# Cross-attention and quantised feed-forward: probabilities turned through device memory, attention one step later

## The reference

```
h    = layernorm(x)
p    = softmax(h ctx^T / 0.72) * mask          # mask: 1.43 where valid, else 0
x1   = x + (p ctx + bias) W
y    = layernorm(x1)
s    = max(max|y|, 1e-6) / 127                 # one value per row
q    = clip(round(y / s), -128, 127)
out  = x1 + (q Wq^T) * s * weight_scale + ffn_bias
```

## Time and profile before

| | |
|---|---|
| time, median of 3 | 327.37 us (326.77 to 328.47) |
| the profiled execution | 327.26 us, span 325.1 us |
| PE, DVE, ACT, POOL busy | 316.5, 288.8, 236.0, 222.9 us |
| share of the chain that ended last: PE | 90% |
| DMA | 55.26 MB, 170 GB/s |
| granted TensorE clock | 1.00 throughout (its upper level, 2.4 GHz) |

### The profile page before, as it was taken

One profiled execution on the slowest core, in us unless ns is written; L12 is line 12 of the kernel. 1 busy time (PEld: TensorE's weight loads), 2 busy tenths in 40 slices (PEclk: granted clock), 3 DMA queues, 4 the chain that ended last, 5 costly groups with the idle time before them and its releaser, 6 DMA issues.

```text
span 325.1 us, 6047 instructions
## 1 busy us (share of the span) xinstructions
PE 316.5 (97%) x1522; PEld 254.8 (78%) x1522; DVE 288.8 (89%) x568; ACT 236.0 (73%) x440; POOL 222.9 (69%) x359
## 2 busy tenths in 40 slices
PE   7999999999999999999999999999999999999993
PEld 7878877778877777887777788877777887777781
DVE  2888889999999999999999999999999999989986
ACT  4466778787778778777777877787787777756651
POOL 3274667677787767678776777877677787766563
PEclk9999999999999999999999999999999999999999
DMA  7997848667485855658595664748667485432002
GB/s 214 272 226 187 196 147 205 190 158 202 146 210 163 219 171 159 196 145 210 161 213 174 161 197 150 203 161 209 178 155 199 144 211 162 126 116 98 33 33 97
DMA packets 69248, 55.26 MB, mean 170 GB/s; under 512 B 21488, under 2 KB 51952, under 8 KB 69232
## 3 DMA queue, kind: packets, MB, share of 16 engines
q1 hardware_dynamic: 61312, 40.65, 49.2%
q10 hardware_dynamic: 7920, 14.42, 13.2%
HBM read 34.87 MB, written 16.25 MB: 157 GB/s over the span
## 4 chain that ended last, share of the span: by engine, by line
PE 90%; DMA 3%; DVE 2%; ACT 1%; SPq 1%; issue 0%; ACTq 0%
PE ps_scores L555 9%; PE ps_scores L557 9%; PE ps_scores L556 9%; PE ps_attn L557 9%; PE ps_attn L555 9%; PE ps_attn L556 9%; PE ps_vw L555 8%; PE ps_vw L557 8%; PE ps_vw L556 8%; PE ps_ffn L716 8%; PE ps_pt L547 4%; DMA x_in<-in_x_dram 2%; DMA ctx_in<-in_ctx_dram 1%; SPq L426 1%; PE ps_pt L543 1%; PE ps_ut L547 1%
## 5 line engine op out<-in xcount | busy, mean ns | idle before, releaser
L1277 POOL TENSOR_TENSOR ct_lo<-ct_raw,ct_hi 128x512 fp32r<-128x512 f32 x28 | 36.2, 1293 | 20.9 <-ACT ct_hi L768 20.9
L555 PE MATMUL ps_vw<-w_hi,ct_hi 128*128 128x512 f32 x116 | 50.5, 435 | 0.0
L555 PE MATMUL ps_attn<-vw_hi,pt_hi 128*128 128x512 f32 x124 | 48.9, 395 | 0.0
L555 PE MATMUL ps_scores<-ct_hi,xt_hi 128*128 128x512 f32 x124 | 48.7, 393 | 0.0
L557 PE MATMUL ps_attn<-vw_hi,pt_lo 128*128 128x512 f32 x124 | 48.4, 391 | 0.0
L557 PE MATMUL ps_scores<-ct_hi,xt_lo 128*128 128x512 f32 x124 | 48.3, 389 | 0.0
L556 PE MATMUL ps_scores<-ct_lo,xt_hi 128*128 128x512 f32 x124 | 48.2, 389 | 0.0
L556 PE MATMUL ps_attn<-vw_lo,pt_hi 128*128 128x512 f32 x124 | 48.2, 389 | 0.0
L1270 POOL TENSOR_TENSOR out_tile<-ffn_out,x_plus 128x512 f32<-128x512 f32 x31 | 40.3, 1299 | 8.6 <-DVE ffn_out L1020 8.6
L557 PE MATMUL ps_vw<-w_hi,ct_lo 128*128 128x512 f32 x116 | 45.4, 391 | 0.0
L556 PE MATMUL ps_vw<-w_lo,ct_hi 128*128 128x512 f32 x116 | 45.3, 390 | 0.0
(11 more groups left out here) (163 smaller groups left out, 776.6 us busy)
## 6 DMA issues: line engine op xcount, KB each, us to landing
x_in<-in_x_dram SPq DMA_DIRECT2D x32, 256.0 KB, 3.1
mask_in<-in_mask_BxSxS_fk_dram SPq DMA_DIRECT2D x32, 256.0 KB, 3.2
norm_rows<-x_norm ACTq DMA_DIRECT2D x30, 256.0 KB, 2.3
x_blocks<-norm_rows SPq DMA_DIRECT2D x120, 64.0 KB, 2.4
ctx_in<-in_ctx_dram SPq DMA_DIRECT2D x56, 128.0 KB, 3.3
out_dram<-out_tile ACTq DMA_DIRECT2D x25, 256.0 KB, 2.5
out_dram<-out_tile SPq DMA_DIRECT2D x6, 256.0 KB, 2.0
ctx_in<-in_ctx_dram SPq DMA_DIRECT2D x4, 256.0 KB, 3.9
```

Source lines behind the costliest of these rows:

```text
L555: nc.tensor.matmul(bank_, lhs_hi(t), rhs_hi(t), start=(t == 0), stop=False)
L1277: nc.gpsimd.tensor_tensor(ct_lo[:, batch_of(n), :, j * P:(j + 1) * P], ct_raw[:, slot(n, 2), :, :], ct_hi[:, batch_of(n), :, j * P:(j + 1) ...
```

## The change

- probs of tiles 3 to 27 are no longer transposed on TensorE. DVE writes them column-interleaved, SP stores them to a new DRAM tensor prob_rows and reads them back as blocks (`store_probs`, `load_probs`, into memory of wq_rows), DVE's block transpose gives pt_raw, and pt_hi and pt_lo are split from there. The last four tiles keep TensorE.
- in the loop PE does scores(d), attend(d-2), V·W of d+4, feed_forward(d-3); quantisation, feed-forward, output and the transposing DMA are a step later as well.
- the mean of x1 comes from a sum that the residual writes out, the mean square of x1 minus its mean from a Square on ACT, in place of bn_stats and bn_aggr.
- xt_lo is made by POOL; the first two small operations of the norm factors become one.
- in SP's step the context pair is issued after x_blocks, the store of probs, x and the mask.
- BY_PE is 29; the bank of V·W alternates between ps_vw and ps_ut; the last tile's integers are rounded, turned and copied in halves, and its output formed by two other operations.

```diff
+            def store_probs(base, n, row):
+                wait_count(sp, probs_ready, base, n + 1)
+                sp.dma_start(prob_rows[bass.ds(row, P), :], probs[:, slot(n, 2), :]) \
+                    .then_inc(prob_rows_stored[slot(n, 2)], 16)
+            def load_probs(base, n, row):
+                quads = prob_rows[bass.ds(row, P), :].rearrange("(a i) d -> i a d", i=BLOCK)
+                wait_bounced(sp, prob_rows_stored, base, n)
+                for b in range(QUADS):
+                    blocks = p_blocks[b * BLOCK:(b + 1) * BLOCK, slot(n, 2), :]
+                    sp.dma_start(blocks.rearrange("i (a c) -> i a c", a=QUADS),
+                                 quads[:, :, b * P:(b + 1) * P]).then_inc(p_blocks_loaded[slot(n, 2)], 16)
...
 # SP, step
-                n = d + 4
-                if n % 2 == 0 and exists(base, n) and ...:
-                    wait_count(sp, ct_raw_ready, base, n - 4 + 2 - PER_BATCH)
-                    load_blocks(ctx_in, ctx_flat, row + n * P, n, 2, ctx_loaded)
                 n = d + 1
...
                     load_rows(base, n, row + n * P)
+                if bounced:
+                    store_probs(base, d - 1, row + (d - 1) * P)
                 n = d + 4
...
                     load_mask(row + n * P, slot(n, 4))
+                n = d + 4
+                if n % 2 == 0 and exists(base, n) and ...:
+                    wait_count(sp, ct_raw_ready, base, n - 4 + 2 - PER_BATCH)
+                    load_blocks(ctx_in, ctx_flat, row + n * P, n, 2, ctx_loaded)
...
+                if bounced:
+                    load_probs(base, d - 1, row + (d - 1) * P)
+                n = d - 3
+                if exists(base, n) and (in_loop(base) or base + n < BY_PE):
+                    turn_integers(base, n)
...
 # PE, loop
+                    attend(d - 2)
+                    next_vw(d + 4)
+                    feed_forward(d - 3)
...
 # ACT, loop
+                    split_next_ctx(d + 4)
+                    round_integers(d - 3)
+                    store_integers(d - 3)
+                    exponentials()
...
+                    split_next_x()
+                    add_up_x(base, d + 4)
+                    split_late_vw(d + 3)
+                    centre(d - 2)
+                    split_bounced_probs(d - 1)
+                    add_up_x1_squares(d - 2)
+                    add_up_squares(base, d + 4)
+                    normalise(base, d + 3)
+                    store_rows(base, d + 3, (base + d + 3) * P)
...
 # DVE, loop
+                    turn_ctx(base, d + 4)
+                    gains(d - 3)
+                    scale_ffn(d - 4)
+                    highest()
+                    turn_x(base, d + 1)
+                    masked()
+                    invert_sum()
+                    residual(d - 2)
+                    turn_probs(d - 1)
+                    split_vw(base, d + 3, vw_bank(base, d + 3))
+                    largest(d - 2)
+                    split_bounced_probs(d - 1)
...
 # POOL, loop
+                    inverse_deviation(d - 3)
+                    split_next_ctx(d + 4)
+                    add_up(d - 4)
+                    add_bias()
+                    split_next_x()
+                    next_mean()
+                    norm_factors(base, d + 3)
+                    add_ffn_bias(d - 2)
```

More of the change, by code:

```diff
@@ L501, in step @@
                             .then_inc(wq_turned, 16)
[L502 to L509, removed]
+                if is_tile(base, d, PER_BATCH - 1):
+                    sp.wait_ge(wq_turned, 16 * NT)
+                if bounced:
[3 more added lines that the diff above has]
+                    turn_integers(base, n)
                 n = d - 4
@@ L516, in step @@
                             .then_inc(last_stored, 16)
-                elif last_batch(base) and not is_tile(base, n, TAIL - PER_BATCH):
+                elif last_batch(base):
                     wait_count(sp, out_ready, base, n + 1)
@@ L898, in step @@
                     centre(d - 1)
[L899 removed]
+                if last_batch(base) and d > 1 and not is_tile(base, d - 2, LAST):
                     round_integers(d - 2)
@@ new lines, in step @@
+                if is_tile(base, d, TAIL):
+                    turn_x(base, d + 1)
+                    gains(d - 3)
+                    scale_ffn(d - 4)
+                    highest()
+                    masked()
+                    invert_sum()
+                    residual(d - 2)
+                    turn_probs(d - 1)
+                    split_vw(base, d + 3, vw_bank(base, d + 3))
+                    largest(d - 2)
+                    split_bounced_probs(d - 1)
+                    split_probs(d)
+                    return
@@ L1113, in step @@
+                if is_tile(base, d, 0):
+                    turn_ctx(base, d + 4)
+                if exists(base, d + 1) and last_batch(base):
+                    turn_x(base, d + 1)
+                if is_tile(base, d - 1, TAIL):
+                    gains(d - 3)
+                    scale_ffn(d - 4)
+                elif is_tile(base, d - 2, TAIL):
+                    gains(d - 3)
+                elif is_tile(base, d, LAST):
                     largest(d - 2)
                 if exists(base, d):
-                    wait_count(dve, scores_done, base, d + 1)
@@ L1157, in step @@
                     x_mean_var(d + 3)
-                if last_batch(base) and d > 0 and exists(base, d):
-                    scale_ffn(d - 3)
+                if last_batch(base) and d > 1 and exists(base, d):
+                    scale_ffn(d - 4)
+                if is_tile(base, d - 1, TAIL):
+                    residual(d - 2)
+                    largest(d - 2)
                 if is_tile(base, d - 1, LAST):
@@ L1226, in _ @@
             pool.wait_ge(identity_ready, 1)
+            for k in range(2):
+                nc.gpsimd.memset(stored_start[:, k:k + 1], 0.0).then_inc(out_stored[k], 16)
             nc.gpsimd.tensor_copy(identity16[:, :], identity[:, :]).then_inc(identity16_ready, 1)
```

463 lines of the change are left out of this document (315 added, 148 removed).

## The result

The changed kernel takes 411.5 us (median of 4, 409.1 to 414.0); the kernel before took 327.9 beside it on the same chip. The ratio is 1.255, 95% interval 1.246 to 1.264. The forecast was 369 us with a range of 347 to 382: the direction and the place were right, the size was not. Some executions of a kernel, whichever it is, run some two per cent longer; medians and ranges here are of all executions, ratios and their intervals leave the slow ones out. The profiled execution took 413.99 us with a span of 412.2.

A forecast was written before the change was run, and what follows sets the result against it. PE bounds the kernel before, at 9.50 us a step; the change makes a two-step ring through SP's late context pair the bound. 327.26 plus 11 × (22.6 − 19.0) = 39.6 plus 2.7 at the exit gives 369.6, said as 369, range 347 to 382.

The forecast's parts named there:

- a ring over two steps: x1_int, SP's issues, ctx landing, DVE's turn, POOL, gains, x1_int: 22.6 us per two steps against 19.0 before; chance 0.82.
- The issues ahead take 6.8 us: On SP, from the end of x1_int to the last issue of the context pair: 6.8 us of the ring.
- the last leg, 2.2: From gains through x_round and x_int to the end of x1_int: 2.2 us of the ring.
- The landing is 3.4: Context pair's DMA lands 3.4 us after its issue, the time taken from the kernel before.
- a landing of 2.2: Short end of the range: ctx lands 2.2 after issue and POOL's way is hidden; ring 20.6 us, total 347.
- contention and the port: Long end of the range: DMA contention and the shared DVE/POOL port add 1.1; ring 23.7 us, total 381.
- POOL's way: From DVE's turn of the context pair through POOL's operations to gains of the odd step: 10.2 us of the ring.
- At the entry the first ctx load covers it: Entry to the loop: the extra step's work is missing there, but the first ctx load covers it.
- The exit: +2.7 forecast: Behind the loop: one more attention (2.7) and feed-forward (0.86), less 0.9 of integer transposes: +2.7 us.
- PE busy about 305: Sign in the changed kernel's profile: PE busy about 305 us (316.5 − 11.9) in a span of 367.
- PE keeps the pace: Rival: ctx lands in time, so only PE's saved work counts, 9.06 us a step, 315.4 us in total; chance 0.09.
- POOL's 8.2 forecast: POOL's work per step: 8.2 us, fitting under PE's 9.06 with little to spare.

The follow-up runs named there:

- e2: Changed kernel with the context pair first in SP's step, still behind the wait for x1_int: 354.4 us, ratio 1.084.
- e4: Kernel before with only SP's order changed, the context pair behind x_blocks, x and mask: 346.7 us, ratio 1.058.
- e5: Changed kernel with the context pair moved ahead of x and mask, still behind x_blocks and the store: 385.8 us, ratio 1.181.
- e1: Changed kernel with the context pair issued before SP's wait for x1_int and the transposing DMA moved behind the pair: 350.1 us, ratio 1.072.
- e8: e1 with SP's output stores of the last steps issued one step later, behind x_blocks and mask: 345.4 us, ratio 1.055.
- e17: e8 with probs store and mask load issued by ACT behind vw_hi, and POOL's inverse deviation ahead of its sum of x1 and ffn_bias: 333.3 us, ratio 1.019.
- e7: e1 with DVE writing probs in plain order instead of column-interleaved, so attention is of permuted columns: 347.4 us, ratio 1.063.

## Why the prediction was right in direction and wrong in size

- **The pair behind the wait for x1_int closes a ring over two steps: right.** DVE waits twelve times, 73.4 us (50 to 60 forecast), POOL's rstd is ahead of q_range in the odd steps (15.8 us over 13), DVE never waits for the read-back, and PE's share of the chain that ended last fell from 90% to 7%. e2, e4 and e5 came in the ranges that the ring gave, and in e1 the waits for the pair went, though not all the time. In the laps DVE took 8.5 to its next turn_ctx, as forecast (8.4).
- **"The issues ahead take 6.8 us": right to 0.1.** So was the last leg, 2.2. On average the laps have 6.9.
- **"The landing is 3.4": the term of the ring that failed most.** That row belonged to a pair issued first in its step. Behind x_blocks, store, x and mask it took 3.9 to 5.35, 4.6 on average: 1.2 a lap, 13 us. I had put a landing of 2.2 at one end of the range and "contention and the port" at 1.1 for both together at the other. With the leg below, 0.6 a lap, and 0.1 of the issues, this makes 24.5 for the usual lap in place of 22.6: 11 × 1.9 = 21 us. The upper end of the ring, 23.7, was below the usual lap too.
- **POOL's way, 10.2 forecast, 10.76 measured (10.8 on average, 6 us in all).** The norm factors took 1.43 from start to start in place of 1.04, the small operation behind xt_lo 0.28 in place of 0.15. The last norm took 0.57 while DVE's pt_lo ran beside it (200.63 to 201.31), and 0.19 or so the earlier trace rows otherwise. pt_lo itself took 1.08 once and 0.68 once in this lap. The Trainium skill's page "SBUF — State Buffer" (the shared port pair) says that a DVE operation with two inputs in SBUF and a GpSimd operation that reads SBUF exclude each other, and these rows agree; it was priced for large operations, and the small ones of POOL are held as well. Over the run thirteen of 32 pt_lo took 1.0 to 1.8; in the loop they stand ahead of DVE's wait for the pair, so the ring didn't pay for them.
- **Back edge: a term that was not in the sum.** Two laps of 28.2 in place of 24.5: 7 us.
- **"At the entry the first ctx load covers it": wrong, 7.9 us.** The first pair too was issued behind x_blocks, store, x and mask, and DVE waited 9.6 for it.
- **The exit: +2.7 forecast, 11.2 measured.** I counted PE's extra work. SP's wait for out_tile ahead of the last blocks is 2.5 of the missing 8.5 (e8). The rest, about 6, I put down to the longer chain from attention to output with one step more in flight; no run tests that.

The sum now is: 369.6 + 21 + 7 + 7.9 + 8.5 = 414, and the profiled execution took 413.99. These terms are read off the trace, so that they add up is no test. It shows where the 44 us are: half in the usual lap, the other half in three places that the range had no room for.

- **"PE busy about 305": wrong, 337.** The instructions were fewer, but longer. Behind the stall of this lap the granted clock fell to its lower level. The window 197.40 to 201.00 (start:end, length, busy of PE, PEld, DVE, ACT, POOL, clock, DMA share, GB/s):

```profile
197.40:201.00 3.60, 3.60 (x10) 2.05 (x9) 3.56 (x9) 3.34 (x8) 3.31 (x6) 0.53 0.85 226
```

0.53 of 2.4 GHz is near the level of 1.2 GHz; the V·W products begin 0.43 apart there, 0.23 just before. PE had stood still for 3.8 us before this batch. The ring and not PE sets the lap, so this should have cost nothing more; no run tested that, nor what the clock costs in e1 and its kin (0.965 to 0.98 on average in e1 and e8, against 1.00 before).
- **The rival "PE keeps the pace", 315: false, and for a second reason that I didn't see.** Even with the pair in time (e1) it is 350, since POOL's order holds rstd, and with it x1_int, the transposing DMA and the feed-forward, and in the other steps pt_lo. Without it (e17) the steps are 9.26 to 9.4, with POOL's step just above PE's, and not 9.06. POOL's 8.2 forecast left out what DVE holds of its small operations, and its wait for ACT.
- The rearranged write of probs takes 1.09, which I had bounded by 0.4 and put at nothing. In e7, on the early pair, it is worth 3 us at most; in the changed kernel itself it lies on no leg of the ring.

## What to carry to other kernels

A load that stands behind a wait in an in-order queue closes a ring through everything that the wait hangs on; price such a ring leg by leg, and take the landing of the last leg with the transfers that will be in front of it, not from a row where it went first. When a ring is broken, look for the next before counting the gain: here bounds lay on one another, at 411, 345 to 350 and 333 us, and single reliefs of engines that were merely busy moved 3 us at most, until the order on POOL was right. When a total comes out as expected, look whether its parts did: e5's did not. Work that moves a step later has its price at the exit as well.

## What the runs showed of the hardware

- The slowest of four DMAs of 128 KB landed 3.2 to 4.7 us (mean 3.6) after its issue when they stood first in SP's step, 3.9 to 5.35 (mean 4.6) behind x_blocks, store, x and mask on the same queue, and 3.2 to 4.9 (mean 4.0) behind x_blocks and store.
- Over the back edge of SP's loop it took 1.9 us from the last issue to the next, or 4.4 to 4.9; with the longer, the instruction queue had 21 packets in place of 10 to 12. Bodies of 72 to 96 issues and one of 112 (318 instructions in the trace) had the short one, others of 112 (288) the long one. What decides is open.
- A DVE write of 512 columns in interleaved order took 1.05 to 1.09 us, in plain order 0.66. The sum that the residual writes out costs a further instruction of 0.08.
- POOL's one-column operations took 0.57 to 0.67 in place of 0.19 where DVE read two operands from SBUF beside them, and such a DVE operation up to 1.8 in place of 0.68 beside POOL's x_plus.
